# An image's first convolution unit, formed by GpSimd from x1 beside the addition

## What is computed

```python
x = x + L0(_gn(x))     # layernorm over channels, 1x1 and depthwise 3x3, channel attention, 1x1 projection
x = x + L1(_gn(x))     # call the first sum x1
# L1: out = concat(conv1x1, conv3x3, conv5x5, conv3x3 dilated by 2); return conv1x1(out, wf)
```

## Time and profile before

| what | us |
|---|---|
| median of 3 runs | 1769.56 |
| lowest and highest run | 1764.85, 1773.46 |
| the profiled execution | 1766.19 |
| its span in the trace | 1764.4 |
| TensorE busy, matmul (13429 instructions) | 1674.1, 95% |
| VectorE busy | 1502.6, 85% |
| ScalarE busy | 1012.0, 57% |
| GpSimd busy | 541.0, 31% |

### The profile page before, as it was taken

The page is one execution under the profiler, slowest core; times in us unless marked ns, Lnnn a source line. Parts: engine busy times, 40 slices in busy tenths (PEclk is TensorE's granted clock), DMA queues, the critical chain, the costliest instruction groups (busy, mean ns, idle before and its releaser), DMA issues.

```text
span 1764.4 us, 40341 instructions
## 1 busy us (share of the span) xinstructions
PE 1674.1 (95%) x13429; PEld 1578.1 (89%) x13429; DVE 1502.6 (85%) x1950; ACT 1012.0 (57%) x1638; POOL 541.0 (31%) x351
## 2 busy tenths in 40 slices
PE   5989988999999999899999999999999999989998
PEld 5989857999989996899999997799999999689998
DVE  5788848999868877999978886899997887699996
ACT  2746656564366667656438566755636666664551
POOL 5799910223254000122328000032235500012222
PEclk9999978999999997999999999799999999899999
DMA  7012113566611210566650220266661021055453
GB/s 186 0 32 67 46 31 79 152 166 170 167 46 32 72 40 1 127 176 163 171 142 0 67 71 6 54 156 167 171 176 56 27 71 46 1 121 142 123 151 98
DMA packets 101196, 166.24 MB, mean 94 GB/s; under 512 B 40010, under 2 KB 74411, under 8 KB 100940
## 3 DMA queue, kind: packets, MB, share of 16 engines
q1 hardware_dynamic: 77932, 138.95, 31.1%
q10 hardware_dynamic: 23168, 26.04, 4.6%
HBM read 52.20 MB, written 25.17 MB: 44 GB/s over the span
## 4 chain that ended last, share of the span: by engine, by line
PE 50%; issue 17%; DVE 17%; POOL 9%; DMA 2%; ACT 2%; SPq 2%; DVEq 1%; POOLq 0%; ACTq 0%
PE ps L865 14%; PE ps L712 12%; PE ps L733 6%; PE ps L735 5%; PE ps L734 5%; PE ps L761 3%; PE ps L796 3%; DVE region L1474 3%; DVE region L1408 2%; DVE region L1505 2%; POOL region L611 2%; DVE region L1523 2%; POOL W L552 1%; POOL W L571 1%; DVE region L1536 1%
## 5 line engine op out<-in xcount | busy, mean ns | idle before, releaser
L865 PE MATMUL ps<-region,W 128*96 128x256 f16 (+4 forms) x7156 | 803.3, 272 | 15.6 <-DMA region<-region 15.6
L865 PEld LDWEIGHTS ps<-region,W 128*96 128x96 f16 (+2 forms) x7156 | 780.6, 122 | 31.4 <-issue 22.0
L621 POOL TENSOR_TENSOR region<-region 96x528 f32<-96x528 f32 (+1 forms) x72 | 96.4, 1343 | 924.9 <-DVE region L1474 923.6
L1278 DVE TENSOR_TENSOR region<-V,band 128x2322 f32<-128x2322 f32 (+2 forms) x104 | 260.8, 2518 | 59.9 <-PE ps L735 57.6
L1058 ACT ACTIVATE region<-region 96x1584 f16<-96x1584 f32 (+2 forms) x88 | 110.8, 1301 | 331.2 <-DVE region L1419 317.9
L733 PE MATMUL ps<-region 128*128 (+1 forms) x1152 | 229.1, 281 | 12.6 <-DVE region L1278 9.2
L735 PE MATMUL ps<-region 128*128 (+1 forms) x1152 | 223.7, 276 | 0.0
L734 PE MATMUL ps<-region 128*128 (+1 forms) x1152 | 223.4, 276 | 0.0
L712 PE MATMUL ps<-proj,region 96*128 96x240 f32 x1024 | 210.7, 369 | 8.3 <-DVE region L1536 8.3
L712 PEld LDWEIGHTS ps<-proj,region 96*128 96x128 f32 x1024 | 196.1, 192 | 22.0 <-issue 8.7
L1505 DVE SCALAR_TENSOR_TENSOR region<-ps,small,region 96x768 f32<-96x768 f32 (+1 forms) x220 | 203.7, 989 | 12.6 <-PE ps L865 11.3
(11 more groups left out here) (196 smaller groups left out, 2075.5 us busy)
## 6 DMA issues: line engine op xcount, KB each, us to landing
region<-region SPq DMA_DIRECT2D x116, 247.5 KB, 4.0
region<-in_x_dram SPq DMA_DIRECT2D x128, 192.0 KB, 2.4
out_dram<-region SPq DMA_DIRECT2D x40, 576.0 KB, 4.2
region<-region ACTq DMA_DIRECT2D x72, 247.5 KB, 2.5
X<-in_x_dram SPq DMA_DIRECT2D x30, 576.0 KB, 6.0
region<-region SPq DMA_DIRECT2D x36, 247.4 KB, 4.9
X<-in_x_dram SPq DMA_DIRECT2D x19, 384.0 KB, 11.3
region<-region SPq DMA_DIRECT2D x24, 185.6 KB, 3.5
```

The costliest lines, as they stand in the source:

```text
L865: last = mm(o, w, src, start=k == 0, stop=k == len(steps) - 1, skip_group_check=split and ck > 0)
L1278: v.tensor_tensor(T[:, i, 3 * c:3 * c + m].rearrange("p m (i j) -> p m i j", j=3), taps.broadcast_to([P, m, BW // 3, 3]), mask.broadcast_t ...
```

## The change

First unit of each image:

- GpSimd has a new function `first_planes`, called in each image in front of its first `differences`. Once the first set of four tiles of x1 is added (and the attention products of the second set are done, whose strips lie where the planes go), it forms the planes of blocks 1 to 4 from X itself, without norm: the planes are differences, so the shift drops out and the scale can come later. These are 18 steps, 16 subtractions or additions and two fills. Then it waits for VectorE's row of block 0 (which needs the group mean, because of the zero rows at the border) and does six more steps.
- VectorE forms block 0's rows (X less the mean) and two of its planes, and adds the mean twice to point 4's plane, which is no difference; these steps stand between the steps of the statistics. Its `planes(0, 0)`, the norm at line 1560 and the fills for the first unit are gone.
- ScalarE's `rows_normed(0, 0)` is gone. Its high parts take the scale SA; their order is: part 0, then (after GpSimd's last steps) part 1's planes, the copies of part 0, part 1's sums, the norm of the second unit's rows, the copies of part 1. Its first set of squares is done in two halves. `lows` of the first unit multiplies by SA.
- TensorE's first and third point of the first unit (`g` = 0 and 2) read 96 partitions of the parts as made (`hi` and `low`) instead of 128 with placed ones: 48 products instead of 37. The placed parts are still made, and waited for at `g` = 1 and 3. `keep_warm` ahead of the unit has 10 instead of 40 products.
- The second unit's `lows` on VectorE waits until the third point is done, as the first unit's low parts are now read where the second's will be written. Column sums and rows of the first unit lie in halves of the rings that only the second unit fills.

Weights: the scaling that was GpSimd's first step of the split is done by ScalarE, as five activations in image 1, and TensorE no longer waits for `s_split`; VectorE does, before the first unit's low parts.

Start: the statistics of the first three loads are done in front of VectorE's setup steps.

TensorE's and VectorE's loops over the images are unrolled (`for b in range(B)`); their inner loops stay.

```diff
-    pool.wait_ge(s_fold, N_COPIES + 5)
-    pool.wait_ge(s_dv, N_WSC)
-    plain = W32[:, FOLDED_AT:FOLDED_AT + 5 * 5 * C]
-    step(pool.tensor_scalar(plain, plain, col(WSC), None, ALU.mult))
+    pool.wait_ge(s_fold, N_COPIES + 6 + 5)
...
+    def first_planes():
+        _, _, pln, yb, cs = buffers(0)
+        rows = X[:, 0:(4 * OR + OR) * W].rearrange("p (r j c) -> p r c j", j=HC, c=2)
+        taps = lambda t, c, count: rows[:, t + 1:t + 1 + 4 * OR, c] \
+            .rearrange("p (k t) j -> p k t j", t=OR)[:, :, 0:count]
+        slots = lambda x, end, c: pln[:, 1:5, x * RW:end * RW] \
+            .rearrange("p k (t c j) -> p k t c j", c=2, j=PC)[:, :, :, c, 1:1 + HC]
+        plane = lambda k, end, x: pln[:, k:end, x * RW:(x + 1) * RW]
+        twice = f32at(Y2F_AT + YF * RW, 5 * RW).rearrange("p (k e) -> p k e", k=5)
+        def done(n):
+            pool.wait_ge(s_fp, b * NFP + n + START)
+        def column_sums(k, end, x, y):
+            pairs = pln[:, k:end, x * RW:y * RW].rearrange("p k (q e) -> p k q e", e=RW)
+            dst = cs[0][:, k:end, 0:PC] if x == 3 else cs[1][:, k:end]
+            pool.tensor_tensor(dst.rearrange("p k (q j) -> p k q j", j=PC), pairs[:, :, :, PC:RW],
+                               pairs[:, :, :, 1:1 + PC], ALU.add).then_inc(s_fp, 1)
+        def take(dst, a, d):
+            pool.tensor_tensor(dst, a, d, ALU.subtract).then_inc(s_fp, 1)
+        def point_0_and_inf(k, end, n):
+            done(n)
+            take(twice[:, k:end], plane(k, end, 1), plane(k, end, 0))
+            take(plane(k, end, 2), plane(k, end, 2), plane(k, end, 1))
+            done(n + 2)
+            take(plane(k, end, 0), twice[:, k:end], plane(k, end, 0))
+            take(plane(k, end, 2), plane(k, end, 2), plane(k, end, 1))
+            done(n + 4)
+        pool.wait_ge(s_x1, b * SETS * 2 + 2 + START)
+        pool.wait_ge(s_o, (b * SETS + 2) * AR + START)
+        for c in range(2):
+            take(slots(3, 5, c), taps(2, c, 2), taps(1, c, 2))
+        pool.memset(pln.rearrange("p k (q j) -> p (k q) j", j=PC)[:, :, 0:PC:PC - 1], 0.0).then_inc(s_fp, 1)
+        pool.memset(yb, 0.0).then_inc(s_fp, 1)
+        done(3)
+        take(twice[:, 1:5], plane(1, 5, 4), plane(1, 5, 3))
+        done(5)
+        take(plane(1, 5, 3), twice[:, 1:5], plane(1, 5, 3))
+        for n in (8, 10):
+            for c in range(2):
+                take(slots(4, 5, c)[:, :, 0], slots(4, 5, c)[:, :, 0], taps(1, c, 1)[:, :, 0])
+            done(n)
+        column_sums(1, 5, 3, 4)
+        for c in range(2):
+            take(slots(0, 3, c), taps(2, c, 3), taps(0, c, 3))
+        point_0_and_inf(1, 5, 13)
+        column_sums(1, 5, 0, 3)
+        pool.wait_ge(s_pl0, b * NPL0 + 1 + START)
+        own = yb.rearrange("p r e -> p (r e)")
+        take(pln[:, 0, 0:3 * RW], own[:, 2 * RW:], own[:, 0:3 * RW])
+        point_0_and_inf(0, 1, 19)
+        column_sums(0, 1, 0, 3)
...
+    first_planes()
...
-with pe.Fori(0, B) as b:
+for b in range(B):
...
-    pe.wait_ge(s_split, N_SPLIT)
...
-    keep_warm(0, 40)
+    keep_warm(0, 10)
...
                 if first:
                     pe.wait_ge(s_wt, NPLACES * 16)
-                    pe.wait_ge(s_h, n * NH + 4 + START)
-                    pe.wait_ge(s_firstp[0], (b + 1) * FIRSTP + START)
+                    pe.wait_ge(s_h, n * NH + 2 + START)
                 else:
                     pe.wait_ge(s_dup[1 - i], (b * 5 + k2 + i) * DUP + START)
                     pe.wait_ge(s_h, (n + 1) * NH + START)
                     pe.wait_ge(s_ext[i], (b * 5 + k2 + i) * EXT + START)
                 pe.wait_ge(s_acc, (n - 1) * NACC + 2 + START)
             elif g == 1:
+                if first:
+                    pe.wait_ge(s_h, n * NH + 5 + START)
+                    pe.wait_ge(s_firstp[0], (b + 1) * FIRSTP + START)
+                    pe.wait_ge(s_firstlo[0], (b + 1) * FIRSTLO + START)
...
             if first and g == 2:
+                pe.wait_ge(s_h, n * NH + 6 + START)
+            if first and g == 3:
                 pe.wait_ge(s_h, n * NH + 8 + START)
                 pe.wait_ge(s_firstp[1], (b + 1) * FIRSTP + START)
-            split, late = g == 0 or first and g == 2, []
+                pe.wait_ge(s_firstlo[1], (b + 1) * FIRSTLO + START)
+            unplaced = first and g in (0, 2)
+            split, late = g == 0 or unplaced, []
...
+                if unplaced:
+                    for rt, second in rts:
+                        for x_ in range(KIND_TAPS[ck]):
+                            steps.append((wh[0:C, rt, KIND_AT[ck] + x_, :], window(buffers(0)[1], C, second, x_)))
+                elif ck == 0:
...
-                        pe.wait_ge(s_firstlo[g // 2], (b + 1) * FIRSTLO + START)
+                        pe.wait_ge(s_l, b * UNITS * NL + g + 2 + START)
...
+    with act.If(b < 1):
+        act.wait_ge(s_dv, N_WSC)
+        for k in range(5):
+            act.activation(folded[:, k], folded[:, k], ACT.Copy, scale=col(WSC)).then_inc(s_fold, 1)
...
+    def squared_halves(k, n):
+        for half in range(2):
+            act.wait_ge(s_x1, (b * SETS + k) * 2 + half + 1 + START)
+            squared(k, half, 2, n + half)
+    squared_halves(0, 0)
+    with act.Fori(1, SETS - 1) as k:
         act.wait_ge(s_x1, (b * SETS + k + 1) * 2 + START)
-        squared(k, 0, 1, k)
-    for half in range(2):
-        act.wait_ge(s_x1, (b * SETS + SETS - 1) * 2 + half + 1 + START)
-        squared(SETS - 1, half, 2, SETS - 1 + half)
+        squared(k, 0, 1, k + 1)
+    squared_halves(SETS - 1, SETS)
...
-            for part in range(2):
-                act.wait_ge(s_pl, n * NPL + (3, 7)[part] + START)
-                plain(hi, part)
-                act.wait_ge(s_pl, n * NPL + (4, 8)[part] + START)
-                sums(hi, part)
-                copied(part, 4 * part + 2)
-                if part == 0:
-                    midway()
+            act.wait_ge(s_pl0, b * NPL0 + 4 + START)
+            plain(hi, 0)
+            act.wait_ge(s_pl0, b * NPL0 + 6 + START)
+            act.wait_ge(s_fp, b * NFP + 11 + START)
+            sums(hi, 0)
+            act.wait_ge(s_fp, b * NFP + 23 + START)
+            plain(hi, 1)
+            copied(0, 2)
+            act.wait_ge(s_fp, b * NFP + 24 + START)
+            sums(hi, 1)
+            midway()
+            copied(1, 6)
...
-    rows_normed(0, 0)
...
+statistics(0, 3)
 dve.wait_ge(s_w, NLOADS * 16)
...
-statistics(0, 6)
+statistics(3, 6)
...
+    def first_block_rows():
+        dve.wait_ge(s_fp, b * NFP + 4 + START)
+        v.tensor_scalar(yb.rearrange("p r (c j) -> p r c j", c=2)[:, 2:, :, 1:1 + HC],
+                        X[:, 0:OR * W].rearrange("p (r j c) -> p r c j", j=HC, c=2),
+                        col(MG), None, ALU.subtract).then_inc(s_pl0, 1)
+        first_done(1)
+        own = yb.rearrange("p r e -> p (r e)")
+        v.tensor_tensor(plane0(0, 3, 5), own[:, 2 * RW:4 * RW], own[:, RW:3 * RW], ALU.subtract).then_inc(s_pl0, 1)
+    def first_part():
+        first_done(2)
+        v.scalar_tensor_tensor(plane0(0, 3, 4), plane0(0, 3, 4), -2.0, plane0(0, 4, 5),
+                               ALU.mult, ALU.add).then_inc(s_pl0, 1)
+        dve.wait_ge(s_fp, b * NFP + 10 + START)
+        one = pln0[:, 1:5, 4 * RW:5 * RW].rearrange("p k (c j) -> p k c j", c=2)[:, :, :, 1:1 + HC]
+        v.tensor_scalar(one, one, col(MG), col(MG), ALU.add, ALU.add).then_inc(s_pl0, 1)
+    def first_sums():
+        first_done(4)
+        v.tensor_tensor(cs0[0][:, 0, 0:PC], plane0(0, 3, 4)[:, PC:RW], plane0(0, 3, 4)[:, 1:1 + PC],
+                        ALU.add).then_inc(s_pl0, 1)
+        one = pln0[:, :, 4 * RW:5 * RW]
+        v.tensor_tensor(cs0[0][:, :, PC:2 * PC], one[:, :, PC:RW], one[:, :, 1:1 + PC], ALU.add).then_inc(s_pl0, 1)
+    yn = buffers(1)[3]
     v.memset(col(MG), 0.0)
     dve.wait_ge(s_x1, (b + 1) * 2 * SETS + START)
     moments(st, tsums[:, 0:2 * SETS], MEAN2, MEAN)
     assert st.n == N_MEAN2
...
+    first_block_rows()
+    dve.wait_ge(s_xs, (b + 1) * (SETS + 2) + START)
+    link(st, v.tensor_reduce(col(SQ), tsums[:, 2 * SETS:], AX.X, ALU.add))
     link(st, v.scalar_tensor_tensor(col(VG), col(SQ), 1.0 / (H * W), col(VAR), ALU.mult, ALU.add))
     assert st.n == N_VG2
+    first_part()
     dve.wait_ge(s_sqrt, b * 3 + 4 + START)
     link(st, v.reciprocal(col(SA), col(RSTD)))
     st.done(v.scalar_tensor_tensor(col(SBI), col(MG), -1.0, col(SA), ALU.mult, ALU.mult))
     assert st.n == N_AFF2
+    first_sums()
...
         if whole == 1:
+            dve.wait_ge(s_cv, b * UNITS * NCV + 3 + START)
...
+            if whole == 0:
+                v.scalar_tensor_tensor(low[:, :, x:end], src, col(SA), hi[0:C, a:e, x:end],
+                                       ALU.mult, ALU.subtract).then_inc(s_l, 1)
+                return
...
-    v.tensor_scalar(yf[:, 2 + FIRST_ACT:].rearrange("p r (c j) -> p r c j", c=2)[:, :, :, 1:1 + HC],
```

(31 more changed lines are left out.)

115 lines of the change are left out of this document (44 added, 71 removed).

## The result

| | before, same chip | after |
|---|---|---|
| median of the runs | 1768.41 us | **1741.9 us** (1739.97 to 1744.47) |
| ratio | | **0.985** (95% interval 0.982 to 0.988) |
| profiled execution | 1766.2 | 1741.5 |
| its span | 1764.4 | 1739.2 |

The change saves 26.5 us, 1.5%. Forecast was 12.6 us, 1757. The direction holds and the time lies just inside the low end of the range (1741 to 1770); the size is off by a factor of two. "Before" has one run more here than in the table of the kernel before, hence its other median.

A forecast was written before the change was run, and what follows sets the result against it. The prediction took TensorE's standing at hand-overs as the bound: the weight split once, addition to convolution in each image. Start -2.4, split -12.2 and first unit +2.0 sum to -12.6, from 1769.56 to 1757 us; range 1741 to 1770.

The forecast's parts named there:

- Start, -2.4: Before image 1: six statistics passes go ahead of VectorE's setup, so the aggregate comes at 41.3 instead of 43.75; -2.4 us.
- Split, -12.2: Image 1, after the depthwise stage: TensorE no longer waits for GpSimd's weight split, so image 1 runs as image 2; -12.2 us.
- The scaling: Weight split: GpSimd's scaling of 8.36 us becomes five ScalarE passes, hidden in 7.37 us of idle; split ends near 218.
- The loops over images unrolled on TensorE and VectorE: Outer loops of both engines: unrolling them costs nothing, as inner loops stay; bounds -1 and +2 us.
- The first unit, +0.5 per image: Between addition and convolution: the second unit's low parts wait for the third point, 721.8 against 721.50; +2.0 us in four images.
- No queueing: Rival, between addition and convolution: VectorE's small steps pass GpSimd, or GpSimd is faster; -28.2 us in all, 1741; chance 0.15.
- The clock: Rival, first unit: TensorE's second or third point pays 1.6 us after waiting; -6.2 us in all, 1763; chance 0.22.
- The split giving nothing: Rival, image 1: another wait, strips or sums of the next image, takes the split's place; 1769 us; chance 0.10.
- the strided inputs as the larger price: Rival, GpSimd's new list: strided inputs cost 3.67 ns an element, +5.5 us on its list; +9.4 in all, 1779; chance 0.10.

The follow-up runs named there:

- the small steps: The changed kernel with five one-element VectorE steps between addition and affine written as operations on one tile with per-partition scalars: 1744.4 us, ratio 0.986.
- that gap filled: The changed kernel with 14 identity products that nobody reads in TensorE's idle 3.3 us ahead of the second unit: 1740.2 us, ratio 0.983.
- the repaired version: The changed kernel with five one-element VectorE steps made single-tile and 14 identity products in TensorE's gap between first and second point: 1738.4 us, ratio 0.983.
- the sides alone: The kernel before with both loops written out, no TensorE wait for the split, scaling on ScalarE, three loads' statistics first; first unit unchanged: 1738.9 us, ratio 0.982.

## Why the prediction was wrong in size

- **Start, -2.4:** right (-2.4), and by the reason given, the last two passes behind TensorE's product (39.98 for 40.0).
- **Split, -12.2:** right (-12.3). The end forecast near 218 came at 219.6, without effect.
- **The scaling.** The prediction says it "goes to ScalarE, as five passes over 480 elements", that the idle ScalarE hides them, and counts its end only for the split. This step failed: the term left out is what the 8.36 us had held on VectorE, and it measured -5.6 us (-6.1 alone). The mechanism stood in the prediction, for small steps in the addition; it was not applied to the longest GpSimd step in the trace, whose neighbour on VectorE read 13.30 us.
- **"The loops over images unrolled on TensorE and VectorE: I cost them at nothing, as their inner loops stay; bounds -1 and +2."** This step failed too: it measured -8.5, outside the bounds, as TensorE's turn of the loop stood on the path. The wait list of before had 8.3 us in three waits, 3.3 the longest, on the first product of an image. I passed over them as a wait for VectorE.
- **The first unit, +0.5 per image:** mechanism right at the marks that count (affine 9.1 for 9.4, second point 19.6 for 19.5, low parts 29.2 for 29.2, then waiting for TensorE). One piece was off without effect: the first point began at 12.6 for 11.9 and took 6.3 us for 5.45 (its first 24 products 3.62 us, 2.83 with the small steps), so that TensorE stood 0.65 us before the second point and not 2. The size is +0.8, as the clock fell in the gap ahead of the second unit; with that gap filled it is +0.1 (894.6 against 894.1).
- **The rivals.** No queueing: refuted by the steps of 1.2 to 1.9 us, though its 1741 is the time that came. Here a right number would have had a wrong reason. The clock: it fell, but not where this rival had it, before the second or third point; it fell ahead of the second unit (4.15 for 2.85), at less than half the price (0.7 us an image, 897.3 against 894.6 in four, for 1.6). The split giving nothing, and the strided inputs as the larger price: refuted; GpSimd's strided pairs of 512 and 768 elements took 1.51 and 2.18 us a step, 2.8 to 2.9 ns an element instead of 3.67, 1.2 us more than priced for the four. Its list ended 1.0 us late.

Forecast plus the two missing terms: -12.6 - 5.6 - 8.5 = -26.7, against -25.2 of the span and -24.7 between the profiled executions.

Not settled: what part of a loop's turn is the fetch of code, what gives back half of the gain behind the filled gap, and whether the first unit's change can gain more than 0.25 us an image; no time here tells the repaired version (1738.4) from the sides alone (1738.9). For use I would take the latter: it is faster than the kernel before, no slower than the changed one, and simpler.

## What to carry to other kernels

When a change bundles a named idea with several small moves, undo them one at a time: here the idea cost 3 us and the small moves saved 30 by the medians, 26 by the spans. Before moving work off GpSimd, read what VectorE does beside it; a step that takes several times its usual length there is part of the price. And an idle gap closed in one place is worth nothing if TensorE arrives early at the next one and stands until its clock falls.

## What the runs showed of the hardware

- The turn of an outer loop on TensorE costs 2.3 to 3.4 us here, with nothing to wait for, and the profile may name an engine that happened to end at that time. Written out it costs nothing; on VectorE its turn was hidden. The loop brings seven more packets of 16 KB on the engine's instruction queue (55 for 48), and behind a turn of 3.26 us the clock was 0.76 over 7 us, where it was 1.00 without the loop.
- Beside one GpSimd step of 8.36 us a VectorE step of two tensors took 8.04 us, where its like took 2.71. Steps of a single element beside GpSimd's additions took 0.6 to 1.9 us instead of 0.16 to 0.22, and 0.21 to 0.27 again once they read one tile and scalars. GpSimd may pay as well: its additions of 192 elements in the weight split, beside the band matrices, took 0.59 or 2.8 us each; no run separates this.
- After 3.5 us of standing, TensorE's granted clock was 0.58 over the next 4 us, of its levels 1.2 and 2.4 GHz mostly the lower; with 3.3 us of identity products in the gap it was 1.00.
